# A graph layer's rows kept with features on partitions, its norm as a scale and bias there

## The chip, the cores and the metric

The kernel runs on one core of one Trainium2 chip. The metric is the device time of one launch, in microseconds (us); lower is better. The engines are TensorE (PE; its weight loads are PEld), VectorE (DVE), ScalarE (ACT), GpSimd (POOL) and SyncE (SP), which issues most DMAs. TensorE's clock is granted at one of two levels: the profile's 1.00 is 2.4 GHz and its 0.50 is 1.2 GHz.

## What is computed

One layer over a graph of 6250 nodes with 256 features and 100000 edges, all float32: a graph convolution and a linear attention side by side, then a mixture of experts. The part that the change touches is the graph convolution's end and the sum behind it:

```python
norm = dinv[src_f] * dinv[dst_f]                      # dinv = 1 / sqrt(degree)
out = segment_sum(h[src_f] * norm[:, None], dst_f) + conv_bias      # h = xn @ W
mu = out.mean()                                       # over all nodes and features
xc = out - mu
std = sqrt((xc * xc).mean())
y = xc / (std + EPS) * ln_weight + ln_bias
gnn = where(y >= 0, y, prelu_a * y)
x = x + gnn + mix                                     # then: experts(layernorm(x))
```

The experts take two of eight per node, chosen by a router whose logits are (normed x) @ Wr.

## The kernel before

The program runs in stages with a barrier between them. The **prologue** sorts out the edges, counts degrees, makes `dinv`, norms x and stores it as a table in DRAM. The **aggregation** gathers table rows per edge and sums them by destination into `acc`, which holds the aggregated features with features on partitions (two halves of 128) and nodes along the free axis; the attention runs in the same stage. At its end SP loads the graph weights `gw` and, spread over all partitions, the rows `cbias`, `lnw`, `lnb` (L726 to L730). It leaves the sum of x and the attention in `zT`, also with features on partitions; `o_tile(t)` is its tile t.

The **router stage** (from L1350 on) is what the change rewrites. A row tile is 128 nodes; there are T = 49. It has these parts, in each engine's order of instructions:

- *Products* (`rows`, L1452, and L1613 on VectorE). TensorE multiplies a tile of `acc`, as weights, by `gw` (256 columns): rows on partitions. VectorE multiplies by `dinv` per row, adds `cbias`, writes x_all and takes statistics (L1620). Four PSUM banks go round.
- *Statistics* (L1639 to L1668). VectorE joins the statistics, TensorE sums over partitions with a matrix of ones (L1472, L1473), twice, ScalarE takes a square root, and VectorE makes `aw`, the norm's factor per feature, scales the weights by it (`wx`, L1665), and makes the offset `bx`.
- *Loop over the tiles* (L1502 on TensorE, L1550 on ScalarE, L1590 on GpSimd, L1692 on VectorE). TensorE makes the products again with the scaled weights (`scaled`, L1482: the norm is in the weights); VectorE multiplies by `dinv` and adds `bx` (`shifted`, L1675); ScalarE takes the negative part (L1542); GpSimd adds the shifted rows to `o_tile` (L1588); VectorE adds (1 - a) times the negative part (`finish`, L1681), takes statistics (L1686) and joins them (L1690). TensorE turns the finished row (`flip`, L1491, two transposes), ScalarE copies the turned row out of PSUM (L1548), and TensorE multiplies it by the router weights (`logits`, L1498: two products of 8 columns with the turned row as weights). SP stores the rows and loads the expert weights w2 between the stores, each when the second products have freed its part of `acc` (L1411).
- *Placement* (from L1704). VectorE makes the second norm's factors, waits for all logits (L1724), chooses experts and works out where every row goes, up to L1828. ScalarE norms the rows (L1564), SP stores them and loads w1. A barrier follows.

A float32 product stands in the profile as two instructions, a transpose as one.

The **expert stage** then runs 105 tiles through the experts.

TensorE's order in the loop is

```python
for s in range(T + 5):
    if s < T:
        scaled(s)
    if 0 <= s - 4 < T:
        flip(s - 4)
    if 0 <= s - 5 < T:
        logits(s - 5)
```

## Time and profile before

| | us |
|---|---|
| median of 3 runs | 1374.73 |
| lowest, highest | 1374.25, 1379.48 |
| span of the profiled execution | 1377.2 |
| products, 789.9 to 836.5 | 46.6 |
| statistics, 836.5 to 844.7 | 8.2 |
| loop over the tiles, 844.7 to 926.1 | 81.4 |
| placement, 926.1 to 971 | 45 |

The profiled execution's own time is not given apart from its span. In the whole span PE is busy for 90%, DVE for 70%, POOL for 62% and ACT for 39%. A profile row that is a line of the timeline gives the start in us from the span's start, the time, engine, line, operation, tiles out<-in with partitions x elements, how many were merged, and in brackets the engine's idle time before it with what ended it. Instructions of one engine overlap a little, so the step from one start to the next is what one costs in a stream.

### The profile page before, as it was taken

Reading aid. Unit: us, or ns where it says so; the run is one execution under the profiler, and the core shown is the slowest. Engines: PE = TensorE matmul, PEld = TensorE weight load, DVE = VectorE, ACT = ScalarE, POOL = GpSimd, SP = SyncE. Lnnn points to the kernel's source line nnn. Section 1 sums busy time; section 2 is a strip of 40 time slices with the busy share of each in tenths; the row PEclk is TensorE's granted clock in tenths of the full one; section 3 lists DMA queues with packets and bytes.
Section 4 is the critical chain, followed back from the end, with each engine's and each line's share of the span. In section 5 each row is a group of like instructions: output and inputs, shape, how many; then the busy total and the mean of one; then the engine's idle time right before and its main releaser. Section 6 shows DMA issues by size and latency. Waiting matters only on the chain. (4 is left out here: it accounts for less than half of the span.)

```text
span 1377.2 us, 30864 instructions
## 1 busy us (share of the span) xinstructions
PE 1245.3 (90%) x8354; PEld 1106.3 (80%) x8355; DVE 962.4 (70%) x2966; ACT 539.3 (39%) x1443; POOL 854.3 (62%) x836
## 2 busy tenths in 40 slices
PE   4997688999899999999898797985799999999998
PEld 4984687887788888887787686873699999999997
DVE  8998787887888777778693288998444444444444
ACT  7707301222333333333311101446455555555553
POOL 1294677777777777777777202431376666666665
PEclk9999899999999999999999898995799999999999
DMA  7005333335666666789898400449244444444443
GB/s 245 0 0 183 111 106 103 107 105 172 194 194 199 198 191 202 207 246 277 260 288 261 144 1 16 138 155 318 64 77 66 68 71 69 72 69 70 71 69 42
DMA packets 138148, 186.89 MB, mean 136 GB/s; under 512 B 21438, under 2 KB 116468, under 8 KB 137916
## 3 DMA queue, kind: packets, MB, share of 16 engines
q0 software_dynamic: 43440, 90.29, 28.7%
q1 hardware_dynamic: 94604, 95.40, 21.8%
q8 instruction: 42, 0.69, 0.2%
q14 instruction: 62, 0.51, 0.1%
HBM read 153.16 MB, written 33.41 MB: 135 GB/s over the span
## 5 line engine op out<-in xcount | busy, mean ns | idle before, releaser
L740 POOL DMA_INDIRECT RG<-table,srci x484 | 477.3, 986 | 153.0 <-issue 149.4
L757 PEld LDWEIGHTS ps<-S_t,RG 128*128 128x128 f32 x1936 | 259.2, 196 | 39.0 <-DMA RG<-table,srci 28.6
L757 PE MATMUL ps<-S_t,RG 128*128 128x96 f32 x1936 | 266.4, 278 | 21.6 <-DMA RG<-table,srci 21.1
L780 PE MATMUL ps<-zrow,R 128*128 128x256 f32 (+1 forms) x784 | 221.1, 389 | 15.2 <-DMA zrow<-table 8.7
L2010 POOL DMA_INDIRECT out<-R,S_t x105 | 166.3, 1584 | 99.5 <-DVE R L1980 55.8
L1893 PE MATMUL ps<-R,RG 128*128 128x128 f32 x1680 | 207.3, 277 | 0.0
L1893 PEld LDWEIGHTS ps<-R,RG 128*128 128x128 f32 x1680 | 198.3, 194 | 0.4 <-issue 0.4
L1903 PE MATMUL ps<-R 128*128 x840 | 198.5, 379 | 0.0
L1014 DVE TENSOR_TENSOR R<-R,ps 128x245 f32 (+4 forms) x300 | 142.1, 474 | 73.7 <-PE ps L768 52.5
L1926 ACT ACTIVATE R<-ps,RG 128x128 f32<-128x128 f32 x420 | 120.0, 368 | 175.8 <-PE ps L1893 175.8
L1976 DVE TENSOR_TENSOR R<-ps,R 128x256 f32<-128x256 f32 x105 | 44.6, 425 | 200.8 <-PE ps L1903 200.8
L780 PEld LDWEIGHTS ps<-zrow,R 128*128 128x128 f32 (+1 forms) x784 | 136.9, 192 | 41.2 <-DMA zrow<-table 19.8
L1903 PEld LDWEIGHTS ps<-R 128*128 128x128 f32 x840 | 151.7, 190 | 16.3
L884 ACT ACTIVATE R<-iwin 128x256 f32<-128x256 f32 (+2 forms) x152 | 71.3, 476 | 186.0 <-PE ps L780 174.2
L1998 POOL DMA_INDIRECT R<-ntable,S_t x105 | 104.2, 992 | 41.5 <-issue 29.0
L1935 ACT ACTIVATE RG<-R 128x1028 f32 x105 | 112.8, 1076 | 10.6 <-PEq L76 10.6
L1588 POOL TENSOR_TENSOR R<-R,slot 128x256 f32<-128x256 f32 x49 | 35.9, 733 | 93.5 <-DVE slot L1675 93.5
L455 PE MATMUL ps<-R 128*128 128x49 bf16 x784 | 80.7, 276 | 10.4 <-DVE R L544 10.3
L455 PEld LDWEIGHTS ps<-R 128*128 128x128 bf16 x784 | 72.7, 144 | 18.4 <-DVE R L544 12.2
L1965 DVE TENSOR_SCALAR R<-ps,gamma,beta 128x128 f32<-128x128 f32 x212 | 76.1, 400 | 0.0
L971 DVE TENSOR_TENSOR S_t<-dstrel,iwin 128x384 f32<-128x384 f32 x121 | 66.7, 551 | 0.7
L984 DVE TENSOR_TENSOR R<-R,ps 128x192 f32 x121 | 42.7, 353 | 31.0 <-issue 23.4
(360 smaller groups left out, 1989.9 us busy)
## 6 DMA issues: line engine op xcount, KB each, us to landing
zrow<-table SPq DMA_DIRECT2D x384, 128.0 KB
RG<-table,srci POOLq DMA_INDIRECT x484, 3.3
ntable<-R SPq DMA_DIRECT2D x12, 516.0 KB
table<-RG SPq DMA_DIRECT2D x12, 512.0 KB, 2.9
out<-R SPq DMA_DIRECT2D x12, 512.0 KB, 3.2
R<-in_x SPq DMA_DIRECT2D x6, 896.0 KB, 11.7
R<-in_w SPq DMA_DIRECT2D x8, 514.0 KB, 6.4
slot<-in_x SPq DMA_DIRECT2D x32, 128.0 KB
```

The lines of the kernel that those rows point to most:

```text
L455: last = nc.tensor.matmul(ps[7][:, 0:T], ohlo[k][:, :, c], ohhi[k][:, :, c], start=False, stop=False)
L740: nc.gpsimd.indirect_dma_start(out=grows[:, s, :], out_offset=None, in_=table, in_offset=bass.IndirectOffsetOnAxis(ap=srci[:, ND + q, c:c ...
L757: last = nc.tensor.matmul(window(q % 2)[:, h, :], grows[:, s, h * P:(h + 1) * P], S_t[:, q % 2, c, :], start=c == 0, stop=c == GC - 1)
L780: nc.tensor.matmul(psD[:, 0:D], adj[b % 2][0:n, j, :], zrow[0:n, i % ZR, :], start=j == 0, stop=j == T - 1).then_inc(z_used, 1)
L1014: nc.vector.tensor_tensor(win, win, psK[m % 2][:, 0:T * wide].rearrange("p (j w) -> p j w", w=wide), ALU.add).then_inc(cnt_ok, 1)
L1893: last = nc.tensor.matmul(psH[s % 2][:, h * P:(h + 1) * P], w1r[:, s, k * HID + h * P:k * HID + (h + 1) * P], ur[:, s % 2, k, :], start=k ...
L1903: last = nc.tensor.matmul(psY[s % 2][:, 0:D], hr[:, s % 2, h, :], w2_sb[:, bass.ds(e, 1), h, :].rearrange("p a f -> p (a f)"), start=h == ...
L1926: last = act.activation(hr[:, s % 2, h, :], psH[s % 2][:, h * P:(h + 1) * P], ACT.Gelu, bias=w1r[:, s, KC * HID + h:KC * HID + h + 1])
L1935: act.activation(w1r[:, s, :], w1_sb[:, bass.ds(e, 1), :].rearrange("p a f -> p (a f)"), ACT.Copy).then_inc(c_ok, 1)
L1965: nc.vector.tensor_scalar(ur[:, s % 2, k, :], psX[s % 2][:, k * P:(k + 1) * P], gamma[:, k:k + 1], beta[:, k:k + 1], ALU.mult, ALU.add)
L1998: nc.gpsimd.indirect_dma_start(out=xr[:, t % 4, :], out_offset=None, in_=ntable, in_offset=bass.IndirectOffsetOnAxis(ap=gat[:, t:t + 1], a ...
L2010: nc.gpsimd.indirect_dma_start(out=a_out, out_offset=bass.IndirectOffsetOnAxis(ap=sct[:, t:t + 1], axis=0), in_=yr[:, t % 4, :], in_offset ...
```

## The change

The products are made with the weights on TensorE's side and `acc` as the moving operand, so that rows come out with features on partitions: 13 chunks of four tiles (the last, of one tile, goes first), each in two halves of 128 features. The degree factors then run along the free axis: the prologue turns `dinv`, stores it to DRAM as a row (`drow`), and SP loads it spread over all partitions, chunk by chunk. The bias and the norm are a scale and a bias per partition, so the second products and the scaled weights go. Over spans of 1 to 6 tiles ScalarE makes two parts of the PReLU, a negative one into a buffer (Relu) and a linear one in place (Identity); VectorE adds them (`bend`); TensorE turns each row tile back to rows on partitions (`turn_rows`, two transposes); VectorE adds it to `o_tile` out of PSUM (`row_residual`). `flip` and `logits` stay. GpSimd's residual goes. The joined statistics per tile give way to five operations over all tiles. The expert weights w2 are loaded ahead of the stores. `cbias`, `lnw` and `lnb` are 128 x 2 now and are loaded in the prologue.

```diff
+                for d_, s_ in ((cbias, a_cb), (lnw, a_lnw), (lnb, a_lnb)):
+                    sp.dma_start(d_, s_.rearrange("(k p) -> p k", p=P), allow_slow_non_contiguous=True).then_inc(w_in, 16)
                 sp.wait_ge(slow_ok, 1)
                 sp.dma_start(outside, slowT.rearrange("p g c -> p (g c)")).then_inc(slow_out, 16)
+                sp.wait_ge(dt_ok, 1)
+                sp.dma_start(drow.rearrange("(t p) -> t p", p=P), dinvT).then_inc(dr_out, 16)
...
+                pe.wait_ge(tr_ev, 6)
+                pe.wait_ge(aff_ok, 1)
+                nc.tensor.transpose(ps[5][0:T, 0:P], dinv[:, :], ident[:, :]).then_inc(dt_ps, 1)
...
+                v.wait_ge(dt_ps, 1)
+                nc.vector.tensor_copy(dinvT, ps[5][0:T, 0:P]).then_inc(dt_ok, 1)
...
-                sp.dma_start(cbias, a_cb.unsqueeze(0).to_broadcast([P, D])).then_inc(late, 16)
-                sp.dma_start(lnw, a_lnw.unsqueeze(0).to_broadcast([P, D])).then_inc(late, 16)
-                sp.wait_ge(pe_done, GQ - 1)
-                sp.dma_start(lnb, a_lnb.unsqueeze(0).to_broadcast([P, D])).then_inc(late, 16)
-                sp.wait_ge(late, 16 * 4)
+                sp.wait_ge(late, 16)
...
+        CT = 4
+        NCH = -(-T // CT)
+        CHUNKS = [NCH - 1] + list(range(NCH - 1))
+        assert (T - 1) % CT == 0 and TAIL % 2 == 0
+
+        def chunk_tiles(c):
+            return min(CT, T - c * CT)
+
+        def feature_rows(c, h):
+            return x_all[:, c * CT:c * CT + chunk_tiles(c), h * P:(h + 1) * P]
+
+        SPANS = []
+        for n in (2, 2, 4, 6, 6, 6, 6, 6, 6, 4, 1):
+            SPANS.append((SPANS[-1][1] if SPANS else 0, (SPANS[-1][1] if SPANS else 0) + n))
+        assert SPANS[-1][1] == T
+        AHEAD = 8
+
+        def span_of(t):
+            return next(k for k, (_, hi) in enumerate(SPANS) if t < hi)
+
+        def by_tile(ap):
+            return ap.rearrange("p (t n) -> p t n", n=P)
...
+            psW = [ps[0], ps[1], ps[3], ps[7]]
+            psF = [ps[6], ps[5], ps[2]]
+            NW, NF = len(psW), len(psF)
...
+                def load_factors(i, c):
+                    if i >= 4:
+                        sp.wait_ge(y_ok, KC * (i - 3))
+                    n = chunk_tiles(c) * P
+                    sp.dma_start(factors[i % 4][:, 0:n], drow[c * CT * P:c * CT * P + n].unsqueeze(0)
+                                 .to_broadcast([P, n])).then_inc(d_in[i % 4], 16)
...
                 def load_w2(e):
                     at = e * HC * D
-                    sp.wait_ge(px_ok, min(T, -(-(at + HC * D) // P)) if at + HC * D <= N else T)
+                    end = -(-(at + HC * D) // (CT * P))
+                    sp.wait_ge(pr_ok, KC * (end + 1 if end < NCH else NCH))
...
+                for i, c in enumerate(CHUNKS):
+                    load_factors(i, c)
+                for e in range(NX):
+                    load_w2(e)
                 for h in range(NB4):
                     store_x1(h)
...
+                def products(i, c, h):
+
+                    u = KC * i + h
+                    if u >= 4:
+                        pe.wait_ge(y_ok, u - 3)
+                    n = chunk_tiles(c) * P
                     for k in range(KC):
-                        last = nc.tensor.matmul(ps[t % 4][:, 0:D], acc[:, k, t * P:(t + 1) * P], gw[:, k, :],
-                                                start=k == 0, stop=k == KC - 1)
+                        last = nc.tensor.matmul(ps[u % 4][:, 0:n], gw[:, k, h * P:(h + 1) * P],
+                                                acc[:, k, c * CT * P:c * CT * P + n], start=k == 0, stop=k == KC - 1)
                     last.then_inc(pr_ok, 1)
...
+                def total(n):
+                    pe.wait_ge(part, n + 1)
+                    nc.tensor.matmul(ps[7][:, 4 * n:4 * n + 4], ones[:, :], tot4, start=True,
+                                     stop=True).then_inc(whole, 1)
+
                 for n in range(2):
-                    pe.wait_ge(part, n + 1)
-                    nc.tensor.matmul(ps[7][:, n:n + 1], ones[:, :], tot2[:, 0:1], start=True, stop=False)
-                    nc.tensor.matmul(ps[7][:, n:n + 1], ones[:, :], tot2[:, 1:2], start=False,
-                                     stop=True).then_inc(whole, 1)
-
-                pe.wait_ge(wx_ok, 1)
-
-                def scaled(t):
-                    if t >= 2:
-                        pe.wait_ge(v_ok, t - 1)
+                    total(n)
+
+                def turn_rows(t):
+
+                    pe.wait_ge(pre_ok, KC * (span_of(t) + 1))
+                    if t >= NW:
+                        pe.wait_ge(x_ok, t - NW + 1)
                     for k in range(KC):
-                        last = nc.tensor.matmul(psW[t % 2][:, 0:D], acc[:, k, t * P:(t + 1) * P], wx[:, k, :],
-                                                start=k == 0, stop=k == KC - 1)
-                    last.then_inc(px_ok, 1)
+                        last = nc.tensor.transpose(psW[t % NW][:, k * P:(k + 1) * P], x_all[:, t, k * P:(k + 1) * P],
+                                                   ident[:, :])
+                    last.then_inc(row_ps, 1)
 
                 def flip(t):
                     pe.wait_ge(x_ok, t + 1)
-                    if t >= 2:
-                        pe.wait_ge(f_ok, t - 1)
+                    if t >= NF:
+                        pe.wait_ge(f_ok, t - NF + 1)
                     for k in range(KC):
-                        last = nc.tensor.transpose(psF[t % 2][:, k * P:(k + 1) * P], o_all[:, t, k * P:(k + 1) * P],
+                        last = nc.tensor.transpose(psF[t % NF][:, k * P:(k + 1) * P], o_all[:, t, k * P:(k + 1) * P],
                                                    ident[:, :])
                     last.then_inc(f_ps, 1)
 
                 def logits(t):
                     pe.wait_ge(f_ok, t + 1)
                     for k in range(KC):
-                        last = nc.tensor.matmul(psL[:, t * NX:(t + 1) * NX], turned[:, t % 2, k * P:(k + 1) * P],
+                        last = nc.tensor.matmul(psL[:, t * NX:(t + 1) * NX], turned[t % NF][:, k * P:(k + 1) * P],
                                                 wrg[:, k, :], start=k == 0, stop=k == KC - 1)
                     last.then_inc(l_ps, 1)
 
-                for s in range(T + 5):
+                for s in range(T + 4):
                     if s < T:
-                        scaled(s)
+                        turn_rows(s)
+                    if 0 <= s - 3 < T:
+                        flip(s - 3)
                     if 0 <= s - 4 < T:
-                        flip(s - 4)
-                    if 0 <= s - 5 < T:
-                        logits(s - 5)
+                        logits(s - 4)
...
+                def negative_part(m, lo, hi, h):
+                    if m >= NBENT:
+                        act.wait_ge(pre_ok, m - NBENT + 1)
+                    act.activation(by_tile(bent[m % NBENT][:, 0:(hi - lo) * P]), x_all[:, lo:hi, h * P:(h + 1) * P],
+                                   ACT.Relu, bias=bx[:, 1, h:h + 1], scale=aw[:, 1, h:h + 1])
+
+                def linear_part(lo, hi, h):
+                    here = x_all[:, lo:hi, h * P:(h + 1) * P]
+                    act.activation(here, here, ACT.Identity, bias=bx[:, 0, h:h + 1],
+                                   scale=aw[:, 0, h:h + 1]).then_inc(lin_ok, 1)
 
                 def flipped(t):
                     act.wait_ge(f_ps, t + 1)
-                    if t >= 2:
-                        act.wait_ge(l_ps, t - 1)
-                    act.activation(turned[:, t % 2, :], psF[t % 2][:, 0:D], ACT.Copy).then_inc(f_ok, 1)
-
-                for s in range(T + 4):
-                    if s < T:
-                        negative(s)
-                    if 0 <= s - 4 < T:
-                        flipped(s - 4)
+                    if t >= NF:
+                        act.wait_ge(l_ps, t - NF + 1)
+                    act.activation(turned[t % NF], psF[t % NF][:, 0:D], ACT.Copy).then_inc(f_ok, 1)
+
+                act.wait_ge(af_ok, 1)
+                made = 0
+                for s in range(T + 3):
+                    while made < 2 * KC * len(SPANS):
+                        k, part_of = divmod(made, 2 * KC)
+                        lo, hi = SPANS[k]
+                        if lo + (hi - lo) * part_of / (2 * KC) >= s + AHEAD:
+                            break
+                        h, linear = divmod(part_of, 2)
+                        if linear:
+                            linear_part(lo, hi, h)
+                        else:
+                            negative_part(KC * k + h, lo, hi, h)
+                        made += 1
+                    if 0 <= s - 3 < T:
+                        flipped(s - 3)
...
-                def residual(t):
-                    pool.wait_ge(v_ok, t + 1)
-                    nc.gpsimd.tensor_tensor(o_tile(t), o_tile(t), halved(shift[:, t % 4, :]), ALU.add).then_inc(xa_ok, 1)
-
-                for t in range(T):
-                    residual(t)
...
+                def rows(i, c, h):
+
+                    n = chunk_tiles(c) * P
+                    if h == 0:
+                        v.wait_ge(d_in[i % 4], i // 4 * 16 + 16)
+                    u = KC * i + h
+                    v.wait_ge(pr_ok, u + 1)
+                    nc.vector.tensor_tensor(feature_rows(c, h), by_tile(ps[u % 4][:, 0:n]), by_tile(factors[i % 4][:, 0:n]),
+                                            ALU.mult).then_inc(y_ok, 1)
+
+                def row_stats(i, c, h):
+                    v.wait_ge(y_ok, KC * i + h + 1)
+                    some = feature_rows(c, h) if c < NCH - 1 else feature_rows(c, h)[:, :, 0:TAIL]
+                    return nc.vector.bn_stats(stats[:, h * NCH + i, :], some)
...
+                ch.done(nc.vector.tensor_scalar(aw, lnw4, d1, None, ALU.mult))
+                ch.done(nc.vector.tensor_tensor(bx, shift_of.unsqueeze(1).to_broadcast([P, 2, KC]), aw, ALU.mult))
+                ch.done(nc.vector.tensor_tensor(bx, bx, lnb4, ALU.add))
+                v.sem_inc(af_ok, 1)
...
+                def row_residual(t):
+                    v.wait_ge(row_ps, t + 1)
+                    nc.vector.scalar_tensor_tensor(halved(o_all[:, t, :]), halved(psW[t % NW][:, 0:D]), signs[:, 0:1],
+                                                   o_tile(t), ALU.mult, ALU.add).then_inc(x_ok, 1)
...
+                def bend(m, lo, hi, h):
+                    v.wait_ge(lin_ok, m + 1)
+                    here = x_all[:, lo:hi, h * P:(h + 1) * P]
+                    nc.vector.tensor_tensor(here, here, by_tile(bent[m % NBENT][:, 0:(hi - lo) * P]),
+                                            ALU.add).then_inc(pre_ok, 1)
+
+                bends = [(KC * k + h, lo, hi, h) for k, (lo, hi) in enumerate(SPANS) for h in range(KC)]
+                for s in range(T + 1):
+                    while bends and bends[0][1] + (bends[0][2] - bends[0][1]) * bends[0][3] // KC <= s + 3:
+                        bend(*bends.pop(0))
                     if s < T:
-                        shifted(s)
-                    if 0 <= s - 3 < T:
-                        x_stats(s - 3)
-                    if 0 <= s - 4 < T:
-                        x_stats_joined(s - 4)
-                    if 0 <= s - 2 < T:
-                        finish(s - 2)
-                v.wait_ge(ag_ok, T)
-                mean, var = mv[:, :, 0], mv[:, :, 1]
-
-                ch.done(nc.vector.tensor_scalar(sc[:, :], var, 1.0 + EPS, EPS * EPS, ALU.mult, ALU.add))
+                        row_residual(s)
+                    if 0 <= s - 1 < T:
+                        x_stats(s - 1)
+                v.wait_ge(st_ok, T)
+                m_even, q_even, m_odd, q_odd = (stats[:, 0:T, k] for k in (1, 2, 4, 5))
+                nc.vector.tensor_tensor(msum, m_even, m_odd, ALU.add)
+                nc.vector.tensor_tensor(sc[:, :], q_even, q_odd, ALU.add)
+                ch.done(nc.vector.tensor_tensor(sd[:, :], m_even, m_odd, ALU.subtract))
+                ch.done(nc.vector.tensor_tensor(sd[:, :], sd[:, :], sd[:, :], ALU.mult))
+                ch.done(nc.vector.scalar_tensor_tensor(sc[:, :], sd[:, :], D / 4, sc[:, :], ALU.mult, ALU.add))
+                ch.done(nc.vector.tensor_scalar(sc[:, :], sc[:, :], (1.0 + EPS) / D, EPS * EPS, ALU.mult, ALU.add))
```

## Rows read from the trace of the kernel before

**Rows 1.** By stage: stretch, length, busy PE, PEld, DVE, ACT, POOL; clock, DMA, GB/s.

```profile
792.00:836.50 44.50, 43.95 (x200) 38.13 (x199) 39.55 (x100) 0.00 (x0) 0.00 (x0) 0.96 0.00 1
...
836.50:844.70 8.20, 1.68 (x8) 1.51 (x8) 5.45 (x19) 0.20 (x1) 0.00 (x0) 0.69 0.00 0
...
860.00:880.00 20.00, 20.00 (x135) 18.02 (x133) 20.00 (x53) 9.02 (x26) 9.48 (x13) 1.00 0.43 133
```

**Rows 2.** Timeline, end of products to the loop's start: start, length, engine, line, operation.

```profile
835.99 0.48 DVE L1615 SCALAR_TENSOR_TENSOR R<-ps,dinv,RG 128x256 f32<-128x256 f32 x1
...
837.16 1.45 DVE L1639 BATCH_NORM_AGGREGATE small<-RG 128x2 f32<-128x288 f32 x1
...
841.04 0.50 PEld L1472 LDWEIGHTS ps<-small,ones 128*128 128x128 f32 x2 [1.32 <-DVEq L1652]
...
841.42 0.55 PEld L1473 LDWEIGHTS ps<-small,ones 128*128 128x128 f32 x2
...
843.94 0.69 DVE L1665 TENSOR_TENSOR RG<-RG,slot 128x512 f32<-128x512 f32 x1
...
844.74 7.06 PE L1482 MATMUL ps<-RG,R 128*128 128x256 f32 x20 [2.69 <-DVEq L1666]
...
845.29 0.42 DVE L1668 TENSOR_TENSOR RG<-RG 128x256 f32<-128x256 f32 x1
```

**Rows 3.** Timeline, TensorE and VectorE, one tile of the loop.

```profile
872.18 0.49 DVE L1675 SCALAR_TENSOR_TENSOR slot<-ps,dinv,RG 128x256 f32<-128x256 f32 x1
...
872.20 0.51 PE L1498 MATMUL ps<-RG,zrow 128*128 128x8 f32 x4
...
872.56 1.11 PE L1482 MATMUL ps<-RG,R 128*128 128x256 f32 x4
...
872.58 0.42 DVE L1686 BATCH_NORM_STATS2 RG<-R 128x6 f32<-128x256 f32 x1
...
873.51 0.38 PE L1491 MATMUL ps<-ident,R 128*128 128x128 f32 x2
...
873.71 0.48 DVE L1675 SCALAR_TENSOR_TENSOR slot<-ps,dinv,RG 128x256 f32<-128x256 f32 x1
```

**Rows 4.** Timeline, end of the loop.

```profile
923.41 0.30 DVE L1690 BATCH_NORM_AGGREGATE RG<-RG 128x2 f32<-128x6 f32 x2
...
926.07 7.97 ACT L1564 ACTIVATE R<-R,zs_b,zs_s 128x256 f32<-128x256 f32 x16 [1.80 <-DVEq L1713]
...
926.12 0.57 DVE L1724 TENSOR_TENSOR R<-ps,zs_s 128x392 f32<-128x392 f32 x1
```

**Rows 5.** Timeline, TensorE's weight loads at the first z tile.

```profile
111.79 0.29 PEld L464 LDWEIGHTS ps<-ident,RG 128*128 128x128 f32 x2 [3.46 <-ACT RG L330]
```

**Rows 6.** Timeline, a pair of transposes in the expert stage, at clock 0.50.

```profile
980.99 0.64 PE L1883 MATMUL ps<-ident,R 128*128 128x128 f32 x2
```

**Rows 7.** Timeline, end of the aggregation.

```profile
782.66 0.33 SPq L730 DMA_DIRECT2D RG<-in_lnb  x1
...
786.06 0.36 DVE L984 TENSOR_TENSOR R<-R,ps 128x192 f32 x1 [2.61 <-PE ps L757]
```

**Rows 8.** The page's costliest groups, a wide activation: busy, mean ns.

```profile
L1935 ACT ACTIVATE RG<-R 128x1028 f32 x105 | 112.8, 1076 | 10.6 <-PEq L76 10.6
```

**Rows 9.** Busy time by stretch, as in rows 1, around changes of TensorE's clock.

```profile
845.00:849.70 4.70, 4.70 (x12) 3.71 (x13) 1.65 (x4) 0.83 (x2) 1.30 (x2) 0.50 0.01 3
...
949.00:967.00 18.00, 17.55 (x90) 11.93 (x89) 17.05 (x20) 10.65 (x21) 4.99 (x7) 0.50 1.04 344
...
975.50:982.90 7.40, 6.81 (x29) 6.07 (x30) 2.93 (x12) 3.33 (x7) 3.58 (x4) 0.50 0.35 92
...
116.00:136.00 20.00, 17.67 (x82) 8.04 (x80) 20.00 (x62) 19.35 (x40) 8.05 (x20) 1.00 0.78 263
...
726.90:730.30 3.40, 1.17 (x8) 1.12 (x9) 0.00 (x0) 0.92 (x2) 2.49 (x4) 1.00 0.82 254
...
730.30:733.70 3.40, 2.69 (x10) 2.05 (x10) 1.81 (x5) 0.00 (x0) 2.54 (x3) 0.50 0.53 167
```

More of the change, by code:

```diff
@@ new lines, in _ @@
+                        nc.vector.tensor_tensor(lnb4, lnb.unsqueeze(1).to_broadcast([P, 2, KC]), pair, ALU.mult)
+                        for k in range(KC):
+                            last = nc.vector.bn_aggr(joined[:, k, 1, :], stats[:, k * NCH, :])
+                        ch.done(last)
+                    last = row_stats(i, c, h)
+                ch.done(last)
+                means, variances = joined[:, :, :, 0], joined[:, :, :, 1]
+                whole4 = tot4.rearrange("p (h a) -> p h a", a=2)
```

157 lines of the change are left out of this document (67 added, 90 removed).

## The prediction

> **What bounds the kernel now.** I read the busy time by stage first, then the stage that the change rewrites in order of time, then the same view for every place where TensorE's granted clock changes. The stage runs from 789.9 to 971 us and has three parts: the graph products (to 836), the statistics (to 844.7), and the loop over 49 row tiles (to 926), behind which one vector chain leads to the experts.
>
> In the products TensorE is full: 43.95 us of 44.5 [rows 1], 196 products of 256 columns, 0.22 us each. VectorE needs less.
>
> The statistics are one chain of small vector steps, 837.16 to 844.74 [rows 2]. TensorE stands nearly idle there, and its clock falls from 1.00 (2.4 GHz) to 0.50 (1.2 GHz): 0.69 in the mean of 836.5 to 844.7 [rows 1].
>
> In the loop TensorE is full again, 20.00 of 20.00 us at 1.00 [rows 1]. A tile takes 1.53 us, the step from one L1675 to the next [rows 3]: four products of 256 columns 0.87, two transposes 0.22, and four router products of only 8 columns, each with a weight load of 128 columns, 0.45. VectorE is full beside it, but TensorE's stream has no gap either, so it is a bound of its own. From the loop's first product (844.74) to the first vector step that needs the last router product (926.12) it is 81.4 us [rows 2, 4].
>
> **The change part by part.** *Prologue and aggregation: 0.* The turn of the degree factors, its copy and its store are queued on TensorE, VectorE and SP ahead of the first z tile; TensorE stands idle for 3.46 us at this point [rows 5], and one transpose with its copy takes about 1 of them (two transposes take 0.64 at 1.2 GHz [rows 6]). Without that cover it would cost this 1 us. The three small loads added on SP push back the store behind them, whose waiters come only after the whole count of degrees. The three loads taken off the end of the aggregation cost nothing now: the last is issued at 782.66, and VectorE's last add starts at 786.06 [rows 7], so a landing of about 3 us, as far as the two rows leave room, ends first. If it didn't, the gain would be under 1 us.
>
> *Products: 0.* Thirteen chunks in two halves: 96 products of 512 columns and 8 of 128. No row has 512 columns. By columns they cost 0.43 each, and 96 x 0.43 + 8 x 0.11 = 42.4 us, what 196 x 0.2165 comes to now. If a wide product saved the start of a second one, 1 us less; nothing speaks for more. VectorE pays per unit a multiply and a statistics step of 512: 256 further columns cost 0.27 (L1668 to L1665 [rows 2]), so 0.75 + 0.69, less overlap 1.3 us, under TensorE's 1.73. The factor loads are issued four ahead; the first may keep VectorE waiting, but TensorE has four banks to fill, 4 us of products, before it feels that. Behind the last product VectorE still has one multiply and two statistics steps, 2.0 us instead of the 1.17 from 835.99 to 837.16 [rows 2]: +0.8.
>
> *Statistics: -1.6.* The long aggregate (1.45) becomes two of a quarter of its input and a small add: -0.6. One sum product in place of two, twice: -0.7 (the second pair of loads starts 0.38 behind the first [rows 2]). One more small step: +0.2. The 512-column weight scaling and a 256-column one (1.2 us from their first to TensorE's start) become three tiny steps: -0.6. Sum -1.7, and I take -1.6 (bounds -2.5 and 0). With the tail the loop's start comes 0.8 us earlier.
>
> *The loop.* The second products go (0.87 per tile on TensorE); two more transposes come. The residual on GpSimd goes, and with it the stretched vector step. ScalarE makes two parts, each with a scale and a bias per partition: 16 such of 256 columns took 7.97 us, 0.50 each [rows 4]; a further column costs at most 1.08 / 1028 = 0.00105 us (L1935 [rows 8]), so 1.04 for 768, 4 x 1.04 / 6 = 0.69 per tile, and the copy of the turned rows at most another 0.50. VectorE pays 0.40 for the row (872.18 to 872.58: a step starts 0.08 before the one ahead of it ends) and 0.34 for its statistics [rows 3]; the add of 768 columns costs 0.42 + 2 x 0.27 [rows 2], 0.88 less overlap, 2 x 0.88 / 6 = 0.29 per tile: 1.03. TensorE pays four transposes and four router products: 4 x 0.109 + 4 x 0.112 = 0.88 **at 2.4 GHz**. At 1.2 GHz two transposes follow each other at 0.214 (0.64 for two, of which one alone takes 0.42 [rows 6]), and four weight loads of 128 columns with products of one column took 841.04 to 841.97, about 0.21 each [rows 2]: 4 x 0.214 + 4 x 0.213 = **1.71 us per tile**, more than today's 1.53. So the loop hangs on the clock.
>
> *Which clock.* It is 0.50 when the loop starts, as now. Now the loop opens with products of 256 columns back to back, at 0.50 from 845 to 849.7 [rows 9], and then has 1.00. The change takes just these away. What is left is transposes and router products. The trace has two stretches like them. From 116 to 136 TensorE did transposes alone, at 1.00 [rows 9]. From 949 to 967 it was busy for 17.55 of 18 us with products behind a 128-column weight load each, and stayed at 0.50 all the while [rows 9]. At 1.2 GHz half of the new loop's 1.71 us are weight loads for products of 8 columns; I take the second stretch as the nearer, because it too is a full engine whose time goes into weights, and because the clock has also fallen amid work: 0.50 from 730.3 on, behind 3.4 us with 1.17 busy [rows 9]. So 1.2 GHz it is, with 2.4 as the other end.
>
> The Trainium skill (TensorE: Matmul & The Clock Gate, Part 4: PE-mode transpose) says that the full clock does not engage for transposes, which speaks against this change outright: by it the loop could not leave 1.2 GHz and would cost what I forecast. The trace doesn't agree with it as it stands, since the transposes from 116 to 136 ran at 1.00; by that row alone the loop would gain 18 us.
>
> *The loop at 1.2 GHz.* ScalarE opens with twelve parts; tile 4 can be turned when the third span (4 tiles) has been added. Its last part ends at 8 x 0.50 + 4 x 0.77 = 7.1 us, and VectorE, with a row and a statistics step queued ahead, ends that add at 8.4. From there TensorE is the bound: 44 tiles x 1.71 = 75.2. At the start of each of six spans of six tiles the second half's add (0.96) stands in VectorE's queue behind the row and statistics of the tiles before, so TensorE's next turn waits 0.26 for the turn to come out (0.64 - 2 x 0.214, and 0.05 to pass on) + 0.40 + 0.33 + 0.96 + 0.05 = 2.0 us while it has work for 1.28: 6 x 0.72 = 4.3. Behind the last turn come four flips and five sets of router products: 0.43 + 4 x 0.43 + 5 x 0.85 = 6.4. Sum 8.4 + 75.2 + 4.3 + 6.4 = **94.3 us** against 81.4: +12.9. The aggregates per tile go from VectorE, and the five small steps in their place (+1.0) end at about 93 (2.4 us lie between the last aggregate and 926.12 [rows 4]), before the last router product: 0, and 1.0 if that cover is gone.
>
> SP has the expert weights ahead of the stores now; they are read while the products run and are done before the first store. Behind the loop the vector chain sets the pace, so what the loop loses is lost.
>
> **Sum:** -0.8 + 12.9 = +12.1 us. The page gives the profiled execution only its span, 1377.2 us; the median of the three runs is 1374.73, 0.2% below. The difference is put on the median: **1386.8 us**. A measurement of this kernel can tell 0.5% (6.9 us) from no change: the three runs differ by 0.4%.
>
> **The rivals.** *B, the clock rises early in the loop and stays* (faster). For it: the transposes of 116 to 136, and that TensorE at 1.2 GHz would have no pause but at the spans. Then VectorE is the bound: 49 x 0.74 + 14.8 for 22 adds (12 at 0.88, 4 at 0.61, 4 at 0.34, 2 smaller) = 51.1, +3.2 idle before tile 4, +6 x 0.5 where it waits for a turn, +6 x 3 x 0.15 where TensorE (0.88) paces the tiles behind, = 60.0; with the 3.4 of the steps behind 63.4 against 81.4, and -0.8: -18.8, 1355.9 us. It decides where the clock is 1.00 from about the tenth tile.
>
> *C, the clock goes up and down*, since a span's start holds TensorE up and a drop like that of 730.3 follows. Half of the tiles at each: about -3, 1371 us, anywhere from 1360 to 1381.
>
> *D, the second products' going relieves nothing because another engine takes their place at either clock*: ScalarE at 1.2 per tile at most and VectorE at 1.03 would have to be half as dear again. In the profile neither is. It would give 1375.
>
> **How the numbers follow.** The forecast has 0.68 (own range 1381 to 1393: start of the loop 0 to -2.5, the stalls 0 to 7, router products 0.19 to 0.22), B 0.18, C 0.10, D 0.04. Faster by over 0.5% (below 1367.9): B and 0.04 of C, 0.22. Slower (above 1381.6): 0.66 of the forecast. The rest, 0.12, is same. The range of 8 in 10 has the forecast, C, and the upper edge of B: 1357 to 1393.
>
> **What would show it.** Right: the granted clock 0.50 from the statistics to the experts; pairs of weight loads of the transposes lasting as at 1.2 GHz; turned rows 1.7 us apart, with six gaps of 2.4; VectorE and ScalarE with idle time that ends on TensorE; products as long as before; the statistics over a little sooner. Wrong: a clock of 1.00 in the loop with rows 1.0 to 1.2 us apart, where the whole loss turns into B's gain; or a loop whose idle time on TensorE ends on ScalarE or VectorE (D).

## The result and the profile after

The kernel took 1382.99 us (median of 6 runs, 1380.16 to 1385.13) against 1374.82 (6 runs, 1374.08 to 1379.48): +8.2 us by the medians, a ratio of 1.0048 with a 95% interval of 1.0034 to 1.0062. The forecast was 1386.8, from 1357 to 1393, and its likeliest case was a loop at a clock of 0.50; that case came, with two thirds of its loss.

The profiled run took 1380.96 us with a span of 1379.2, so 1.8 us lie outside the span; by the same difference the profiled execution of before, with 1377.2, took about 1379.0 and was one of the long ones. Where the whole time scatters shows in both traces: the products start at 784.40 here and at 789.9 before, and in the runs below anywhere from 782.1 to 790.0. That scatter lies ahead of the stage, so the stage is measured from its own first product; a few us won or lost in the prologue or the aggregation can't be told from it. The text ahead of the prediction has one slip: `zT` holds the sum of x and the attention with rows on partitions, in two halves of 128 features; nothing was worked out from it.

By stage, in the columns of [rows 1]:

```profile
792.00:830.00 38.00, 38.00 (x91) 16.64 (x90) 29.05 (x55) 0.00 (x0) 0.00 (x0) 1.00 0.40 125
830.20:838.00 7.80, 0.97 (x4) 0.80 (x4) 5.79 (x23) 0.20 (x1) 0.00 (x0) 0.74 0.57 203
838.00:846.30 8.30, 2.66 (x10) 1.86 (x10) 4.88 (x12) 8.26 (x14) 0.00 (x0) 0.50 0.00 0
846.30:922.00 75.70, 71.56 (x353) 70.97 (x354) 48.08 (x106) 41.77 (x76) 0.00 (x0) 0.50 0.23 77
```

In the loop (last row) TensorE is busy for 71.56 of 75.7 us at 0.50, VectorE for 48, ScalarE for 42. Before, TensorE and VectorE were both full, at 1.00 [rows 1]. The second products are gone, VectorE has a third of its time free, and the loop is longer all the same. Its shape, in timeline lines as in [rows 3]: the end of the products, ScalarE's first part, the first turn behind the third span, one tile, and the gap at a span.

```profile
830.18 0.69 DVE L1686 TENSOR_TENSOR R<-ps,slot 128x512 f32<-128x512 f32 x1 [0.36 <-PE ps L1509]
...
832.10 0.82 DVE L1722 BATCH_NORM_AGGREGATE small<-RG 128x2 f32<-128x72 f32 x2
...
838.04 0.60 ACT L1598 ACTIVATE slot<-R,small 128x256 f32<-128x256 f32 x1 [1.72 <-DVEq L1752]
...
846.31 0.69 PE L1539 MATMUL ps<-ident,R 128*128 128x128 f32 x2 [2.18 <-DVE R L1766]
...
849.53 0.67 PE L1539 MATMUL ps<-ident,R 128*128 128x128 f32 x2
849.99 0.63 PE L1548 MATMUL ps<-ident,R 128*128 128x128 f32 x2
850.42 0.86 PE L1555 MATMUL ps<-RG,slotb 128*128 128x8 f32 x4
851.13 0.67 PE L1539 MATMUL ps<-ident,R 128*128 128x128 f32 x2
...
852.02 0.86 PE L1555 MATMUL ps<-RG,zrow 128*128 128x8 f32 x4
...
852.57 0.94 DVE L1766 TENSOR_TENSOR R<-R,RG 128x768 f32<-128x768 f32 x1
...
853.56 0.69 PE L1539 MATMUL ps<-ident,R 128*128 128x128 f32 x2 [0.69 <-DVE R L1766]
```

A tile takes 1.60 us (849.53 to 851.13): two transposes 0.46, two more 0.43, the four router products 0.71. At a span the step is 2.43 (851.13 to 853.56): TensorE waits for VectorE's add (L1766), issued at 852.57 behind the tile before. There are six such steps, 2.43 or 2.44 each. The end of the loop, ScalarE's and VectorE's lines and the last router products:

```profile
924.83 0.19 DVE L1784 TENSOR_SCALAR sc<-sc 128x49 f32<-128x49 f32 x1
...
926.51 0.39 ACT L1610 ACTIVATE zrow<-ps 128x256 f32<-128x256 f32 x1 [0.79 <-PE ps L1548]
926.79 0.24 ACT L1630 ACTIVATE sa<-sc 128x49 f32<-128x49 f32 x1
...
926.98 1.00 PE L1555 MATMUL ps<-RG,zrow 128*128 128x8 f32 x4
...
927.06 0.47 DVE L1787 RECIPROCAL zs_s<-sa 128x49 f32<-128x49 f32 x1 [2.05 <-ACT sa L1630]
...
928.88 0.57 DVE L1804 TENSOR_TENSOR R<-ps,zs_s 128x392 f32<-128x392 f32 x1
```

The square root (926.79) has its input at 925.02, but stands on ScalarE behind the copy of the last turned row. The last router product is done at 927.98, but the first vector step on the logits starts only at 928.88, behind the root's chain of vector steps.

From the first product to that step the stage takes 144.5 us; before it took 136.2 (789.92 to 926.12). These +8.3 us agree with the +8.2 of the medians. Behind that step the rest of the span is as long as before, 450.3 us against 451.1, so what the loop loses is not made up.

### The profile page after: what moved, and what is told of

The parts are those of the page before. It is cut to its first block and busy times, and to the rows that moved or that the text cites. A ratio compares the mean times of both kernels' runs of the same rounds, so it can differ in the third digit from the quotient of the medians.

```text
span 1379.2 us, 30248 instructions
## 1 busy us (share of the span) xinstructions
PE 1239.9 (90%) x8161; PEld 1091.5 (79%) x8162; DVE 934.5 (68%) x2859; ACT 556.6 (40%) x1438; POOL 808.8 (59%) x787
## 5 line engine op out<-in xcount | busy, mean ns | idle before, releaser
L751 POOL DMA_INDIRECT RG<-table,srci x484 | 470.5, 972 | 155.5 <-issue 149.8
L768 PEld LDWEIGHTS ps<-S_t,RG 128*128 128x128 f32 x1936 | 256.2, 195 | 29.6 <-DMA RG<-table,srci 19.6
L768 PE MATMUL ps<-S_t,RG 128*128 128x96 f32 x1936 | 261.5, 277 | 14.8 <-DMA RG<-table,srci 14.4
L1662 POOL COPY R<-R 128x8 f32<-128x8 f32 (+1 forms) x13 | 4.0, 325 | 176.9 <-DVEq L1836 155.7
L465 PE MATMUL ps<-R 128*128 128x49 bf16 x784 | 80.7, 276 | 10.4 <-DVE R L557 10.1
```

The source lines that it names most:

```text
L465: last = nc.tensor.matmul(ps[7][:, 0:T], ohlo[k][:, :, c], ohhi[k][:, :, c], start=False, stop=False)
L751: nc.gpsimd.indirect_dma_start(out=grows[:, s, :], out_offset=None, in_=table, in_offset=bass.IndirectOffsetOnAxis(ap=srci[:, ND + q, c:c ...
L768: last = nc.tensor.matmul(window(q % 2)[:, h, :], grows[:, s, h * P:(h + 1) * P], S_t[:, q % 2, c, :], start=c == 0, stop=c == GC - 1)
```

## The experiments

In the table, "stage start" is the first product; "to loop" runs from there to ScalarE's first part (before: to the first second product); "loop" runs from there to the first vector step on the logits; "clock" is the granted clock of most of the loop. Stage times come from each kernel's one profile. Each ratio is to the kernel before as it ran beside that kernel: its medians were 1374.62 for e1 to e4, 1373.67 for e5 to e8, 1374.82 for e9 to e11 and 1375.98 for e12.

| run | time, us | ratio, interval | stage start | to loop | loop | clock |
|---|---|---|---|---|---|---|
| before | 1374.82 | | 789.9 | 54.8 | 81.4 | 1.00 |
| after | 1382.99 | 1.0048 (1.0034 to 1.0062) | 784.4 | 53.6 | 90.8 | 0.50 |
| e1 | 1384.43 | 1.0066 (1.0044 to 1.0089) | 790.0 | 57.6 | 85.4 | 1.00 |
| e2 | 1389.18 | 1.0100 (1.0073 to 1.0127) | 786.8 | 57.7 | 90.7 | 0.50 |
| e3 | 1372.54 | 0.9994 (0.9980 to 1.0007) | 782.4 | 52.8 | 81.0 | 1.00 |
| e4 | 1379.01 | 1.0024 (1.0006 to 1.0041) | 784.4 | 53.8 | 87.6 | 0.50 |
| e5 | 1375.74, 1355.29 to 1380.17 | | 783.1 | 52.6 | 85.5 | 0.50 |
| e6 | 1355.86 | 0.9859 (0.9835 to 0.9883) | 787.3 | 53.8 | 64.8 | 1.00 |
| e7 | 1361.62 | 0.9915 (0.9890 to 0.9940) | 784.4 | 53.4 | 69.7 | 1.00 |
| e8 (before, changed) | 1372.45 | 0.9981 (0.9966 to 0.9997) | 787.6 | 54.4 | 79.0 | 1.00 |
| e9 | 1378.12, one run | | 782.1 | 53.6 | 90.0 | 0.50 |
| e10 | 1404.48 and 1368.06 | | 787.7 | 53.4 | 111.5 | 0.50 |
| e11 | 1357.78 | 0.9877 (0.9853 to 0.9901) | 789.5 | 53.3 | 67.9 | 1.00 |
| e12 | 1355.36 | 0.9855 (0.9826 to 0.9884) | 786.0 | 53.5 | 64.7 | 1.00 |

### First set: is it the clock?

Four kernels. Three give TensorE more to do, into a PSUM bank that nobody reads; the fourth takes the gaps at the spans away.

```diff
-            psF = [ps[6], ps[5], ps[2]]
+            psF = [ps[6], ps[5]]
+            spare = ps[2]
...
+                def dense(count, n):
+                    for _ in range(count):
+                        nc.tensor.matmul(spare[:, 0:n], ident[:, :], dense_in[:, 0:n], start=True, stop=True)
```

`dense_in` is the graph weights, 512 columns. e1 has all of the following, e2 the first part alone (down to `dense(11, 512)`), e3 the last two lines alone:

```diff
-                for n in range(2):
-                    total(n)
+                pe.wait_ge(y_ok, KC * NCH)
+                dense(7, 512)
+                total(0)
+                dense(2, 512)
+                total(1)
+                dense(11, 512)
...
                     if 0 <= s - 4 < T:
                         logits(s - 4)
+                    dense({1: 3, 3: 7}.get(s, 0), 512)
+                    if 4 <= s < T:
+                        dense(1, 256)
```

**e1**

> Of the changed kernel, with TensorE kept busy: 20 products of 512 columns into a bank that nobody reads, in the gaps of the statistics; 10 more while the first spans are made; one of 256 columns behind each tile's router products. Nothing of the result changes; one bank fewer for turned rows. Theory A (the loop is paced by TensorE's work at clock 0.50): the clock is 1.00 through the loop, a tile needs 0.88 + 0.22 us of TensorE, VectorE (1.03 and its share of waits) becomes the bound, and the loop falls from 90.8 to about 63 us: 1355 us, ratio to before 0.986. Rival R1 (the pace is the round trip turn, residual, turn, copy, product between the engines, whatever the clock): clock 1.00 but a loop of 80 us or more: 1372 or above. Rival R2 (transposes don't get the full clock): clock 0.50, each tile 0.43 dearer: about 1402.

**e2**

> The 20 products of 512 columns in the statistics alone, none in the loop. If the loop's own work could hold a clock of 1.00 once it has it, the time is as in the first run of this set without the extra products, 1350 to 1357 us. Theory A (transposes and router products neither raise nor hold it): 1.00 at the first turned tiles, then 0.50 for most of the loop: 1376 to 1383 us. A clock that goes up and down would show between, near 1370.

**e3**

> One product of 256 columns behind each tile's router products alone, nothing in the statistics. Theory A with a clock that stays at 0.50: 45 tiles x 0.43 us dearer, since TensorE has no gap but at the spans: about 1402 us, ratio to before 1.020. If the added products lift the clock on their own, the loop falls as in the first run: 1355 to 1362 us. If TensorE is not what paces the loop, nothing changes: 1383.

**e4**

```diff
-        AHEAD = 8
+        AHEAD = 10
...
-                    while bends and bends[0][1] + (bends[0][2] - bends[0][1]) * bends[0][3] // KC <= s + 3:
+                    while bends and bends[0][1] + (bends[0][2] - bends[0][1]) * bends[0][3] // KC <= s + (4 if s >= 4 else 3):
```

> VectorE adds the two parts of a span one tile earlier from the fifth tile on (ScalarE makes them two tiles earlier), the clock untouched. If the six gaps of 0.86 us on TensorE at the spans are the second half's add standing behind a row and a statistics step in VectorE's queue, they go: 6 x 0.86 = 5.2 us less, 1378 us. If the add waits on ScalarE's parts or the buffers instead, the gaps stay and the time is 1383.

Measured: e1 1384.43, e2 1389.18, e3 1372.54, e4 1379.01. The figure of e2 is the median of three runs; a fourth took 5844.89 us at a mean clock of 1.00, which nothing here explains, and is left out. e1 and e2 missed what was expected of them. **e3 is the plain answer**: TensorE has more to do per tile, and the loop is 9.9 us shorter than in the change. Busy times of e3 by stretch, columns as before, and one tile at either clock:

```profile
838.00:851.50 13.50, 10.48 (x42) 8.78 (x42) 8.03 (x18) 9.96 (x16) 0.00 (x0) 0.50 0.11 39
851.50:914.00 62.50, 58.48 (x438) 52.37 (x436) 46.26 (x106) 38.73 (x72) 0.00 (x0) 1.00 0.29 97
```

```profile
848.65 0.63 PE L1546 MATMUL ps<-ident,R 128*128 128x128 f32 x2
...
851.21 0.53 PE L1546 MATMUL ps<-ident,R 128*128 128x128 f32 x2
...
872.46 0.38 PE L1546 MATMUL ps<-ident,R 128*128 128x128 f32 x2
872.68 0.38 PE L1555 MATMUL ps<-ident,R 128*128 128x128 f32 x2
872.90 0.51 PE L1562 MATMUL ps<-RG,zrow 128*128 128x8 f32 x4
873.26 0.68 PE L1530 MATMUL ps<-RG,ident 128*128 128x256 f32 x2
873.78 0.38 PE L1546 MATMUL ps<-ident,R 128*128 128x128 f32 x2
```

A tile took 2.56 us at 0.50 (848.65 to 851.21) and 1.32 at 1.00 (872.46 to 873.78), with the same instructions. The added products lifted the clock, 16 us into the loop. The gain is smaller than the 1355 to 1362 of the expectation mainly because I had priced the added product at 0.22 us; a float32 product is two instructions, and it costs 0.52 (873.26 to 873.78). For the same reason the products of e1 and e2 overfilled the gaps of the statistics: their way to the loop is 4 us longer than in the change, 57.6 and 57.7 against 53.6. In e1 the ten products in the loop's first gaps also put off the turn of tile 4 to 16.6 us into the loop, against 8.3 in the change, so its loop gains only 5.4 us, and the 4 us eat most of that. The numbers of rival R1 (a round trip of waits) came, a clock of 1.00 with a loop of over 80 us, in e1 and e3. But its mechanism is not what they show: in e3 at 1.00 a tile costs 0.22 + 0.22 + 0.37 + 0.52 = 1.33 on TensorE alone, which is its step, and in e6 below a cheaper product brings the step down to 1.11. R2 (transposes don't get the full clock) falls with the same lines, where a pair of transposes steps 0.22.

e2 shows that a full clock handed to the loop is not kept. Its stretches, from ScalarE's first part to the end of the added work, the time at 1.00 behind it, and the rest:

```profile
844.50:850.50 6.00, 6.00 (x15) 2.66 (x14) 1.70 (x4) 6.00 (x11) 0.00 (x0) 1.00 0.00 0
850.50:860.90 10.40, 6.64 (x51) 5.37 (x49) 8.56 (x20) 7.93 (x13) 0.00 (x0) 1.00 0.23 79
860.90:930.00 69.10, 65.66 (x327) 65.19 (x326) 43.52 (x97) 36.41 (x67) 0.00 (x0) 0.50 0.24 79
```

At 1.00 the loop leaves TensorE gaps, 6.64 busy of 10.4; then the clock falls, and at 0.50 TensorE is busy for nearly all of the rest without rising.

In e4 all later steps are 1.60 us: the six gaps of 0.84 are gone, 5.0 us. But the loop is only 3.3 us shorter, mostly because the step from tile 4 to tile 5 is 3.46 instead of 1.62: TensorE waits for ScalarE's copy of a turned row, which stands behind four parts now (two tiles more ahead was too much at the start):

```profile
847.73 1.01 ACT L1603 ACTIVATE R<-R,small 128x768 f32<-128x768 f32 x1
848.65 0.63 ACT L1610 ACTIVATE zrow<-ps 128x256 f32<-128x256 f32 x2
...
849.07 1.02 PE L1555 MATMUL ps<-RG,zrow 128*128 128x8 f32 x4 [1.47 <-ACT zrow L1610]
```

### Second set: how much does it take, and what is it worth?

The products ahead of the loop are sized to the gaps now, and half a product stands behind a tile. e5 is e4 with all of the following but its last two lines; e6 has these two as well; e7 is e6 with the two lines of e4's diff as they are in the change.

```diff
-                for n in range(2):
-                    total(n)
+                pe.wait_ge(y_ok, KC * NCH - 3)
+                dense(3, 512)
+                total(0)
+                dense(1, 512)
+                total(1)
+                dense(5, 512)
...
                     if 0 <= s - 4 < T:
                         logits(s - 4)
+                    dense({1: 1, 3: 3}.get(s, 0), 512)
+                    if 4 <= s < T:
+                        dense(1, 128)
```

**e5**

> The changed kernel with the earlier adds, and products of 512 columns into an unread bank only before the loop and in the gaps of its first four tiles (13 of them, 0.86 us each by the last set's traces, sized to the gaps), none behind tile 4. Theory A (a loop of transposes and router products doesn't hold the clock, whatever it had before): 1.00 to about tile 8, then 0.50: loop 83 to 87 us, time 1374 to 1379. Rival H (it was the gaps at the spans that made the clock fall in the last set, and the loop at a full pace holds it): 1.00 to the end, a tile at VectorE's 1.03 to 1.15, loop about 64 us, 1356.

**e6**

> The same with one product of 128 columns (half of the last set's) behind the router products of each tile from tile 4 on. By the last set's trace a tile costs TensorE 0.22 + 0.22 + 0.37 at 1.00, and this product 0.26: 1.07 us, beside VectorE's 1.03. If the clock holds, the loop is 8.3 + 44 x 1.15 + 5 = 64 us against 90.8: 1356 us. If half a product is too little to hold it, 0.50 and a tile of 2.1 us: 1399.

**e7**

> The same as the run with the half products, but the adds as late as in the change, so that TensorE stands still for about 0.6 us at each of six spans. If these gaps make the clock fall: 0.50 from the first or second span of six, 1385 or more. If they cost only their own time: 6 x 0.6 = 3.6 us above that run, about 1360.

**e8**: the kernel before, with such products into its bank 6.

```diff
+                pe.wait_ge(y_ok, T - 3)
+                dense(3, 512)
                 for n in range(2):
                     pe.wait_ge(part, n + 1)
...
                                      stop=True).then_inc(whole, 1)
+                    dense(1 + n, 512)
```

> The kernel before, with six such products in the gaps of its statistics. Its loop had 0.50 for its first 4.7 us of full work; with 1.00 from the start these take half: 2.4 us less, 1372.4 us, ratio 0.998. If the clock falls all the same in the statistics, or the products hold up the sums: 1375 or more. It says how much of any gain of the runs above is the clock's and not the change's.

Measured: e6 1355.86 and e7 1361.62 where 1356 and 1360 were expected. e6's loop holds 1.00 throughout; its start, the stretch behind it, and one tile:

```profile
841.00:852.70 11.70, 8.38 (x33) 4.08 (x32) 7.17 (x17) 11.57 (x19) 0.00 (x0) 1.00 0.13 45
852.70:903.00 50.30, 50.24 (x454) 49.91 (x454) 45.67 (x108) 37.38 (x74) 0.00 (x0) 1.00 0.35 116
```

```profile
895.13 0.38 PE L1550 MATMUL ps<-ident,R 128*128 128x128 f32 x2
895.35 0.38 PE L1559 MATMUL ps<-ident,R 128*128 128x128 f32 x2
895.56 0.51 PE L1566 MATMUL ps<-RG,zrow 128*128 128x8 f32 x4
895.93 0.47 PE L1530 MATMUL ps<-RG,ident 128*128 128x128 f32 x2
896.24 0.38 PE L1550 MATMUL ps<-ident,R 128*128 128x128 f32 x2
```

1.11 us per tile, of which 0.31 are the added product; VectorE is close behind with 45.67 of 50.3. In e7 TensorE has steps of 2.15 us at the spans and keeps its clock:

```profile
870.00:880.00 10.00, 9.12 (x83) 8.93 (x81) 8.40 (x19) 7.86 (x14) 0.00 (x0) 1.00 0.32 107
```

e8 came out at 1372.45, where 1372.4 was expected: its first 20 loop instructions take 4.64 us instead of the 7.06 of [rows 2], and its loop is the 2.4 us shorter that were expected. That the whole time fits so well is partly luck: against the kernel before in the same set, 1373.67, the medians differ by 1.2.

```profile
842.05 4.64 PE L1491 MATMUL ps<-RG,R 128*128 128x256 f32 x20 [0.86 <-DVEq L1675]
```

e7 has the change's own schedule. So the change, with the products that hold its clock paid for, is worth 1361.62 - 1372.45 = **-10.8 us where both kernels are kept at 1.00**, and +8.2 where each takes the clock that its own work gets. The intervals of the two ratios leave some 4 us either way. With e4's earlier adds as well (e6) it is 1355.86 - 1372.45 = -16.6; those 5.8 us more (4.9 by the two loops) are the schedule's and not the change's.

e5 has the start without the half products. Its profile fell to 0.50 at 848.8, behind a wait of 1.93 us for ScalarE's copy, and stayed there with TensorE busy all the while:

```profile
845.00:848.80 3.80, 2.23 (x21) 2.23 (x22) 2.53 (x7) 3.80 (x7) 0.00 (x0) 1.00 0.41 138
848.80:918.00 69.20, 69.20 (x349) 69.17 (x349) 46.33 (x108) 38.00 (x72) 0.00 (x0) 0.50 0.27 90
```

But of its ten runs one took 1355.29 us, with a mean clock of 0.959; the other nine took 1372.5 to 1380.2, with 0.934 to 0.942. By time and mean clock, without a profile of that run, rival H holds in one run of ten: the loop can keep a full clock on its own, and mostly doesn't. A tile at 0.50 takes 1.60 us as in the change, so the bank taken from the turned rows costs nothing there. A median over such runs says little, so no ratio is given.

### Third set: raising and holding, and the end

**e9**: the change, with the square root ahead of the last two copies.

```diff
+                    if s == T + 1:
+                        act.wait_ge(root_in, 2)
+                        act.activation(sa[:, :], sc[:, :], ACT.Sqrt).then_inc(root_ok, 1)
                     if 0 <= s - 3 < T:
                         flipped(s - 3)
-
-                act.wait_ge(root_in, 2)
-                act.activation(sa[:, :], sc[:, :], ACT.Sqrt).then_inc(root_ok, 1)
```

> The changed kernel, with ScalarE's square root for the second norm ahead of its last two copies of turned rows instead of behind them. In the profile of the change the root starts at 926.79, behind a copy that ends then, though its input is there at 925.02; VectorE's seven steps behind it end at 928.74, and the last router product at 927.98. If that order is what holds the end, the first vector step on the logits starts at the last router product: the loop is 0.8 us shorter, 90.0 us from ScalarE's first part to that step. If the chain of vector steps is not what it waits for, 90.8 stays. The whole time can't tell 0.8 us.

Measured: a loop of 90.00 us against 90.84, in the one run's profile. VectorE's first step on the logits now waits for TensorE:

```profile
922.76 0.24 ACT L1628 ACTIVATE sa<-sc 128x49 f32<-128x49 f32 x1 [0.56 <-DVEq L1786]
...
925.67 0.57 DVE L1805 TENSOR_TENSOR R<-ps,zs_s 128x392 f32<-128x392 f32 x1 [0.96 <-PE ps L1555]
```

**e10**: e6 without the products ahead of the loop and in its first gaps.

```diff
-                pe.wait_ge(y_ok, KC * NCH - 3)
-                dense(3, 512)
                 total(0)
-                dense(1, 512)
                 total(1)
-                dense(5, 512)
...
-                    dense({1: 1, 3: 3}.get(s, 0), 512)
```

> The run with the half products and earlier adds, without the products ahead of the loop. Theory: what holds a clock of 1.00 is less than what raises it from 0.50, so with TensorE at 0.50 when the loop starts it stays there, a tile costs 1.60 + 0.53 = 2.13 us, the loop is 87.6 + 45 x 0.53 = 111 us, and the time is 1403. Rival: the half products lift it as the whole ones did, after some 15 us: 1358 to 1366.

Measured: two runs, 1404.48 with a mean clock of 0.919 and 1368.06 with 0.950. The profile is of the first. Its loop is 111.5 us (111 was expected), a tile 2.13 us, with TensorE busy all the while at 0.50:

```profile
853.00:950.00 97.00, 97.00 (x456) 97.00 (x457) 48.53 (x110) 39.44 (x74) 0.00 (x0) 0.50 0.21 68
```

By time and mean clock both sides of the expectation came, one in each run; the second, which has no profile, would have risen early. Beside e6's row this is the clearest pair: the same instructions per tile, 97 us full at 0.50, and 50 us full at 1.00.

**e11**: e6 with e9's edit, one copy later (`if s == T + 2`).

> The run with the half products and the products ahead of the loop, with the square root ahead of the last copy of turned rows. There the root's input was ready 0.3 us before the root started: 0.3 us less, which the whole time can't tell: 1355 to 1357 us, ratio 0.986 with a narrower interval. If the clock falls in some of the runs, as in the run without products in the loop, single times of 1370 to 1400 stand among them.

**e12**: e11 with the start of the loop as late as in the change.

```diff
-                        if lo + (hi - lo) * part_of / (2 * KC) >= s + AHEAD:
+                        if lo + (hi - lo) * part_of / (2 * KC) >= s + AHEAD - (2 if s < 9 else 0):
...
-                    while bends and bends[0][1] + (bends[0][2] - bends[0][1]) * bends[0][3] // KC <= s + (4 if s >= 4 else 3):
+                    while bends and bends[0][1] + (bends[0][2] - bends[0][1]) * bends[0][3] // KC <= s + (4 if s >= 9 else 3):
```

> The last run's kernel, with the adds one tile earlier (and ScalarE's parts two tiles earlier) from the tenth tile on instead of the fifth. With them early from the fifth, VectorE waits at the fourth span for parts that ScalarE hasn't made, and the step from tile 4 to tile 5 is 3.36 us where the run with late adds has 1.52. If that is the cause, the step falls to about 1.5, the gap from which the clock once fell is gone, and the loop is 64.8 - 1.8 = 63 us: 1354 us, ratio 0.985. If it is something else, 1356 to 1358 as before.

Measured: e11 1357.78 (1357.24 to 1362.36), e12 1355.36 (1353.18 to 1361.15). In e11's profile, which is of its slowest run, the clock fell at 855.8, behind the step of 3.36 us from tile 4 to 5, and was back at 862.7; four tiles took 1.6 to 2.1 us. In that step TensorE waits for ScalarE's copy:

```profile
853.71 0.61 PE L1566 MATMUL ps<-RG,zrow 128*128 128x8 f32 x4 [1.93 <-ACT zrow L1624]
```

e6 has the same step of 3.36 us with the same wait of 1.93 (849.39 to 852.75), and its clock stayed at 1.00. In e12 that step is 1.52, as expected, but two later ones are 2.15 and 1.74: the loop is 64.7 instead of 64.8, and the 1.8 us aren't gained. The cause named was half right: it was ScalarE's copy behind its own parts, as this line and e4's show, not VectorE. e6, e11 and e12 all beat both kernels, by 1.2 to 1.5% against the kernel before; between them nothing can be told.

## Why the prediction was right, and where its sizes were off

**The deciding step held**: the clock stays at 0.50 from the statistics to the experts, TensorE is the bound, and what the loop loses is lost. The reason given held as well: a full engine whose time goes into weight loads and transposes didn't raise its clock, by the mean clocks in none of six runs. But the choice was a judgement between two stretches of [rows 9] that point opposite ways, and e5 and e10, which differ little from the change, show how near the other side was: by time and mean clock one run of each went that way. The Trainium skill (TensorE: Matmul & The Clock Gate, Part 4: PE-mode transpose) says that the full clock does not engage for transposes. As it stands e6's rows disagree: a pair of transposes steps 0.22 us at 1.00, for 50 us on end. A dense product stands behind every tile there, but from 116 to 136 of the kernel before [rows 9] transposes alone had 1.00 for 20 us as well. What does agree is the change itself, and e5's profile, where little but transposes and router products was left and the clock stayed at 0.50.

**Prologue, aggregation and products, forecast 0.** The prologue and the aggregation can't be read more finely than the scatter of the first product. VectorE waited 2.27 us for the first degree factors, and TensorE ran on. The 88 instructions from 792.13 took 38.01 us, 0.432 each for 512 columns (forecast 0.43; 96 x 0.43 + 8 x 0.11 is 42.2 and not the 42.4 of the prediction, and its "products" are instructions, two to a product). From the first product to the last multiply it is 45.8 us against 46.1.

**Statistics, forecast +0.8 and -1.6.** The last multiply and its statistics took 1.92 us (830.18 to 832.10; forecast 2.0, before 1.17), and from there to the loop it was 5.94 against 7.58: -1.6. With the products' 0.3 the loop starts 1.2 us sooner.

**The loop, forecast 94.3, measured 90.8.** Tile 4 is turned 8.27 us into it (8.4). The term that was mis-sized is **the price of the router products at 1.2 GHz**: I took 0.213 each from the sums over partitions [rows 2], where the loads stand alone. They cost 0.178 (0.71 for four). The row itself, 0.93 for four, gives 0.23 and not 0.21, so it was still further off than the figure taken from it. The nearer row stood beside it: four router products step 0.36 from 872.20 to 872.56 [rows 3], which doubled is 0.72; I had put 0.45 there and 0.87 on the products, whose step is 0.95. The sum 1.53 hid the wrong split. So a tile is 1.60, not 1.71: 44 x 0.11 = 4.8 us too much. The span gaps were 6 x 0.84 = 5.0 (4.3), and behind the last turn it took 7.0 (6.4): the five router sets there were cheaper too, but **the small steps' cover was gone**: I had put them at 0 or 1.0 by TensorE's end and left out that the root, which needs them, stands behind a copy on ScalarE. That cost 0.8 to 0.9, and e9 took 0.8 of it back. Together 8.3 + 70.4 + 5.0 + 7.0 = 90.7.

**The rivals.** B's price, 1355.9, is near what e5's one run with the clock up took, 1355.29, but partly by luck: e5 has e4's earlier adds and a start at 1.00, which B had not. The kernel as written showed it in none of its six runs: their mean clocks are 0.929 to 0.932. C, up and down, is seen in e11 and not in the change. D falls: at 1.00 VectorE and ScalarE hold 1.11 us a tile. The bound of 0.5% lies inside the measured interval, so of the three chances slower (0.66) and same (0.12) can't be told apart; the mechanism can.

**Open** is what makes the clock fall or rise. e7 kept it through steps of 2.15 us; e11 lost it behind one of 3.36, and e6 kept it through the same one; e5 lost it behind the same wait of 1.93 us in its profile and, by its mean clock, kept it in one run of ten. So a gap of this size goes with the fall without deciding it.

## What to carry to other kernels

Removing dense products from an engine that is full can lose, if the products were what kept its clock up: cost the loop that is left at both clocks before counting their time as saved, and look in the trace for a full stretch of the same kind of work and the clock that it had. If what is left is transposes and small products behind full weight loads, compare the change with the clock held, by cheap dense products into a spare bank in the gaps ahead of the loop and behind each tile. And take the price of an instruction from the row of the same stream at the other clock rather than from a lonely one of the same shape.

## What the runs showed that was not expected

One loop has two lasting states: with the same instructions, e10's TensorE is full for 97 us at 0.50 and e6's for 50 us at 1.00, and by their times and mean clocks runs of one kernel can go either way (e5: one of ten at the full clock; e10: one of two). Work that nobody reads made the kernel 1.3 to 1.5% faster (e7: 0.9915 against 1.0048 as ratios to before, 1361.62 against 1382.99 us). And the scatter of this kernel's whole time, some 10 us between single runs of before (1370.46 to 1382.68 of 23), lies to a good part ahead of the stage: in the fourteen profiles its first product comes anywhere within 8 us, and from the first vector step on the logits to the end it is 449.7 to 452.3 in all of them. So effects of one microsecond are read from the stage, not from the time.
